# Values of the global attention begun two units at a time behind the first half of the next unit's scores, with five half slots for its probabilities and three packed slots for those of the local attention

## The reference

```python
x = x + _L0_conv_ref(_gn(x), ...)   # global attention
x = x + _L1_conv_ref(_gn(x), ...)   # local attention

# layer 0, per image and head (12 heads of 16 channels, S = 1024 positions)
scores = q @ swapaxes(k) * SCALE + (rel_h + rel_w)      # 1024 x 1024
out = softmax(scores) @ v                               # then w_proj, b_proj

# layer 1: 7 x 7 neighbourhood mask, and 16 registers that every query sees
scores = where(mask_cat, q @ swapaxes(k_cat) * scale, NEG_INF)   # 1024 x 1040
out = softmax(scores) @ v_cat                           # then out_w, out_b
```

## Time and profile before

| | |
|---|---|
| median of 3 runs | 4896.54 us |
| profiled execution | 4902.5 us |
| its span, first to last instruction | 4900.8 us |
| mean granted TensorE clock | 0.951 of full speed |
| TensorE matmuls busy | 4491.2 us, 92% of the span |
| VectorE busy | 3079.3 us, 63% |
| ScalarE busy | 2608.5 us, 53% |
| DMA, mean | 79 GB/s |

### The profile page before, as it was taken

How to read it: one execution, slowest core, us unless ns; L and a number is a source line. 1 busy time by engine, 2 the same in 40 slices (tenths; PEclk the granted TensorE clock), 3 DMA queues, 4 the chain that set the end, 5 groups by cost and what they waited for, 6 DMA issues and landing times.

```text
span 4900.8 us, 97559 instructions
## 1 busy us (share of the span) xinstructions
PE 4491.2 (92%) x32598; PEld 2291.5 (47%) x32598; DVE 3079.3 (63%) x5558; ACT 2608.5 (53%) x3955; POOL 892.5 (18%) x1901
## 2 busy tenths in 40 slices
PE   5879999999999999999999999999999999999998
PEld 3334453544535454453544535455454544535444
DVE  3736667665675656667566675656657566676654
ACT  1533556555564555556555564555646555565564
POOL 3112111222202212121212202212021121102111
PEclk7888999999999999999999999999999999999999
DMA  6334242443414433253433424433144432424401
GB/s 126 83 73 86 49 104 62 99 90 70 89 39 106 87 87 71 53 108 70 99 79 70 88 52 99 94 73 84 44 106 81 99 79 48 101 62 99 87 14 40
DMA packets 235869, 386.05 MB, mean 79 GB/s; under 512 B 58396, under 2 KB 133728, under 8 KB 235360
## 3 DMA queue, kind: packets, MB, share of 16 engines
q1 hardware_dynamic: 189280, 266.13, 23.8%
q10 hardware_dynamic: 21504, 75.51, 7.6%
q0 software_dynamic: 24576, 37.80, 4.8%
HBM read 227.79 MB, written 88.08 MB: 64 GB/s over the span
## 4 chain that ended last, share of the span: by engine, by line
PE 75%; DVE 9%; SPq 5%; issue 5%; DMA 5%; ACT 2%; DVEq 0%; ACTq 0%; POOL 0%
PE P L1135 15%; PE P L1153 14%; PE P L1094 13%; PE P L958 6%; PE P L959 6%; DVE mx L901 5%; PE P L1071 5%; PE P L1185 4%; PE P L1206 4%; PE P L1102 3%; DMA QA<-queries 2%; PE P L1178 1%; SPq L507 1%; DMA biases<-xn 1%; DVE mxc L907 1%
## 5 line engine op out<-in xcount | busy, mean ns | idle before, releaser
L901 DVE TENSOR_REDUCE mx<-P 128x1 f32<-128x512 f32 x3072 | 1923.2, 682 | 471.2 <-PE P L1094 467.9
L771 ACT ACTIVATE probs<-P 128x1024 f32<-128x1024 f32 x1536 | 1507.5, 1022 | 777.7 <-PE P L1153 777.0
L1094 PE MATMUL P<-K,AR 96*128 96x256 f16 x6144 | 1093.1, 282 | 42.9 <-DMA AR<-biases 26.7
L1153 PE MATMUL P<-AR,K 113*128 113x512 f16 x3072 | 924.8, 383 | 14.1 <-DMA AR<-mrow 13.6
L907 DVE TENSOR_REDUCE mxc<-P 128x1 f32<-128x336 f32 (+1 forms) x1536 | 648.2, 474 | 307.6 <-PE P L1103 304.0
L787 ACT ACTIVATE probs<-P 128x320 f32<-128x320 f32 (+3 forms) x1632 | 618.1, 436 | 405.2 <-PE P L1206 340.0
L1135 PE MATMUL P<-probs,V 128*17 128x512 f32 x6144 | 817.2, 604 | 9.9 <-ACT probs L771 9.9
L1094 PEld LDWEIGHTS P<-K,AR 96*128 96x128 f16 x6144 | 541.7, 99 | 566.9 <-DVE mx L901 198.3
L1153 PEld LDWEIGHTS P<-AR,K 113*128 113x128 f16 x3072 | 216.9, 98 | 676.6 <-ACT probs L771 517.8
L1206 PE MATMUL P<-A,K 113*128 113x320 f16 (+2 forms) x1536 | 447.1, 306 | 12.9 <-ACT probs L787 12.1
L1102 PE MATMUL P<-K,A 112*128 112x320 f16 (+1 forms) x1536 | 400.4, 295 | 53.4 <-DVE mx L901 35.8
(11 more groups left out here) (122 smaller groups left out, 3705.4 us busy)
## 6 DMA issues: line engine op xcount, KB each, us to landing
AR<-biases SPq DMA_DIRECT2D x384, 256.0 KB, 7.7
AR<-queries ACTq DMA_DIRECT2D x96, 512.0 KB, 5.8
biases<-xn SPq DMA_DIRECT2D x192, 256.0 KB, 2.9
AR<-queries ACTq DMA_DIRECT2D x96, 256.0 KB, 8.5
K<-oraw POOLq DMA_DIRECT2D x384, 64.0 KB, 4.8
xin<-in_x_dram SPq DMA_DIRECT2D x16, 768.0 KB, 10.5
queries<-oraw SPq DMA_DIRECT2D x384, 32.0 KB, 4.8
QA<-queries SPq DMA_DIRECT2D x192, 64.0 KB, 5.1
```

Source lines behind the costliest of these rows:

```text
L771: nc.scalar.activation(probs[:, u % RING, j:j + 2, :], P[:, b:b + 2, :], ACT.Exp).then_inc(p_done[0], 1)
L901: V_.reduce_max(mx[:, n // 2, n % 2:n % 2 + 1], bank, AX.X).then_inc(used, 1)
L1094: last = mm(bank[:, QD * (v % 2):QD * (v % 2) + QD], AR[0:ROWS_MAX[0], part % SLOTS, v, c, j, 128 * q:128 * q + 128], K0[0:ROWS_MAX[0], h, ...
L1153: last = mm(P[:, j, :], K0[0:ROWS, h, 128 * kt:128 * kt + 128], AR[0:ROWS, p % SLOTS, kt // 2, :, j, :], start=True, stop=True)
```

## The change

1. In the global attention, the values are no longer issued one unit at a time behind a unit's second step. `values_due(step)` says what is due behind a step: behind every fourth step from 4 to 88 (the first step of a unit) the two units before it; behind steps 91, 93 and 95 one unit each; and the last one behind the loop.
2. `probs` is used as half units. `slot_of(step)` gives each step one of five slots up to step 84, four in `probs` and the fifth in `xres`, and one of the four in `probs` from step 85 on. `left_by(step)` is the step whose slot this one takes; ScalarE waits until the values of that step's unit have been used.
3. Since `xres` is lent out, the input image is loaded into it at step 90 in place of step 32, when 43 units have been used (at step 88), and ScalarE waits ahead of the first exponential until the image before has left `xres`.
4. In the local attention `probs` is packed into three slots of the units' true width (PACKED), and the values are issued by `values_due_local(g, u, j)`, behind the first head of a unit: of unit 0 behind unit 2's first head, of units 1 and 2 behind unit 3's, 3 and 4 behind unit 5's, 5 and 6 behind unit 7's, 7 and 8 behind the next group's unit 0.

```diff
-RING = 2
+PACKED = 1280, 1408, 1408
+FIFTHS = 85
+RELOAD = 90
...
+def values_due(step):
+
+    if step % 4 == 0 and 4 <= step < FIFTHS + 4:
+        return [step // 2 - 2, step // 2 - 1]
+    if step % 2 and step > FIFTHS + 4:
+        return [step // 2 - 1]
+    return []
+
+
+def slot_of(step):
+
+    return step % 5 if step < FIFTHS else (step - FIFTHS) % 4
+
+
+def left_by(step):
+
+    return step - 5 if step < FIFTHS + 4 else step - 4
+
+
+def values_due_local(g, u, j):
+
+    if j:
+        return []
+    if u == 0:
+        return [(g - 1, 7), (g - 1, 8)] if g else []
+    return {2: [(g, 0)], 3: [(g, 1), (g, 2)], 5: [(g, 3), (g, 4)], 7: [(g, 5), (g, 6)]}.get(u, [])
...
-                    if kind == "main" and L == 0 and step == STEPS[0] // G:
...
+                    if kind == "main" and L == 0 and step == RELOAD:
+                        sp.wait_ge(pv_done[0], im * UNITS[0] + FIFTHS // 2 + 1)
                         sp.dma_start(xres[:], x_t[im]).then_inc(xres_in, 16)
...
                 if kind == "main" and L == 0:
+                    if not is_image(im, 0):
+                        spilled = im * 16
+                        act.wait_ge(mid_out, spilled)
                     for step in range(STEPS[0]):
                         u, j = step // 2, 2 * (step % 2)
-                        if j == 0 and u >= RING:
-                            act.wait_ge(pv_done[0], im * UNITS[0] + u - RING + 1)
+                        if left_by(step) >= 0:
+                            act.wait_ge(pv_done[0], im * UNITS[0] + left_by(step) // 2 + 1)
                         act.wait_ge(st_done[0], im * STEPS[0] + step + 1)
                         b = 2 * (step % 2)
-                        nc.scalar.activation(probs[:, u % RING, j:j + 2, :], P[:, b:b + 2, :],
+                        nc.scalar.activation(half_unit(step), P[:, b:b + 2, :],
                                              ACT.Exp).then_inc(p_done[0], 1)
...
                         last.then_inc(st_done[0], 1)
                         run_jobs(after[step], 0)
-                    if u:
-                        use(u - 1)
+                        for due in values_due(step):
+                            use(due)
                 use(UNITS[0] - 1)
...
                         run_jobs(after[step], 1)
+                        for dg, du in values_due_local(g, u, j):
+                            use(dg * (TT + 1) + du)
                         step += 1
                     ends.append(step)
-                    if full:
-                        use(full - 1)
+                use(UNITS[1] - 2)
                 use(UNITS[1] - 1)
                 jobs_read(after)
```

More of the change, by code:

```diff
@@ L241, in attention_kernel @@
         vreg = sb("vreg", [128, G, 128])
-        probs = sb("probs", [128, RING, GH, 512])
+        probs = sb("probs", [128, 2, GH, 512])
         onorm = probs[:, 0, 0:3, :].rearrange("p a n -> p (a n)").rearrange("p (t c) -> p t c", t=TT)
@@ L245, in attention_kernel @@
         xres = sb("xres", [128, TT, C])
+        fifth = xres[:].rearrange("p t c -> p (t c)")[:, 0:2 * 512].rearrange("p (j n) -> p j n", j=2)
+        packed = probs[:].rearrange("p a j n -> p (a j n)")
         xn = sb("xn", [128, 2, S])
@@ L288, in attention_kernel, with half_unit, local_unit @@
         P = ctx.enter_context(nc.psum_tensor("P", [128, 8, 512], F32))
+        def half_unit(step):
+            slot = slot_of(step)
+            return fifth if slot == 4 else probs[:, slot // 2, 2 * (slot % 2):2 * (slot % 2) + 2, :]
+        def local_unit(full):
+            heads, at = (GH, sum(PACKED[0:full % 3]))
+            u = full % (TT + 1)
+            if u == 0:
+                heads, width = 2, 512
+            else:
+                width = W * (query_rows(u - 1)[1] - query_rows(u - 1)[0])
+            assert heads * width <= PACKED[full % 3]
+            return packed[:, at:at + heads * width].rearrange("p (j n) -> p j n", j=heads)
         def banks(a, n, rows=128):
@@ L546, in stage @@
                 for step, entries in enumerate(after):
-                    if kind == "main" and L == 0 and step == STEPS[0] // G:
-                        if is_image(im, 0):
-                            sp.wait_ge(rows_in, ROWS_IN)
-                            sp.wait_ge(out_in, 16)
-                        else:
-                            moved, stored = im * 4, im * 16
-                            sp.wait_ge(xT_done[1], moved)
-                            sp.wait_ge(nb_done[1], im)
-                            sp.wait_ge(mid_out, stored)
+                    if kind == "main" and L == 0 and step == RELOAD:
+                        sp.wait_ge(pv_done[0], im * UNITS[0] + FIFTHS // 2 + 1)
                         sp.dma_start(xres[:], x_t[im]).then_inc(xres_in, 16)
@@ L781, in stage @@
                             full = g * (TT + 1) + u
-                            if full >= RING:
-                                act.wait_ge(pv_done[1], im * UNITS[1] + full - RING + 1)
+                            if full >= len(PACKED):
+                                act.wait_ge(pv_done[1], im * UNITS[1] + full - len(PACKED) + 1)
                             for j in range(GH if u else 2):
@@ L786, in stage @@
                                 n = W * (query_rows(u - 1)[1] - query_rows(u - 1)[0]) if u else 512
-                                nc.scalar.activation(probs[:, full % RING, j, 0:n], P[:, step % SCORES[1], 0:n],
+                                nc.scalar.activation(local_unit(full)[:, j, :], P[:, step % SCORES[1], 0:n],
                                                      ACT.Exp).then_inc(p_done[1], 1)
@@ L1135, in use @@
                         last = mm(P[32 * j:32 * j + D + 1, 6, :], V[0][:, kt, GH * (p // 2) + j, :],
-                                  probs[:, u % RING, j, :], start=(kt == 0), stop=(kt == TT - 1))
+                                  half_unit(2 * u + j // 2)[:, j % 2, :], start=(kt == 0), stop=(kt == TT - 1))
                     last.then_inc(pv_done[0], 1)
@@ L1170, in use @@
                     pe.wait_ge(p_done[1], im * STEPS[1] + ends[full])
-                    slot = full % RING
+                    unit = local_unit(full)
                     if full == 0:
@@ L1177, in use @@
                         for half in range(2):
-                            last = mm(P[:, 6 + half, :], vreg[:, g, :], probs[:, slot, half, :],
+                            last = mm(P[:, 6 + half, :], vreg[:, g, :], unit[:, half, :],
                                       start=True, stop=False, skip_group_check=True)
@@ L1185, in use @@
                                 last = mm(P[32 * j:32 * j + D + 1, 6 + half, a - 512 * half:b - 512 * half],
-                                          V[1][:, u - 1, GH * g + j, :], probs[:, slot, j, a - lo:b - lo],
+                                          V[1][:, u - 1, GH * g + j, :], unit[:, j, a - lo:b - lo],
                                           start=False, stop=(u == HALF_UNITS[half] - 1), skip_group_check=True)
```

## The result

| | before | after |
|---|---|---|
| median | 4895.58 us (4 runs, 4892.41 to 4898.04) | 5116.85 us (4 runs, 5109.57 to 5127.25) |
| profiled execution | 4902.5 us | 5109.57 us |
| its span | 4900.8 us | 5107.0 us |
| mean granted TensorE clock | 0.951 | 0.941 |

The change makes the kernel slower: ratio 1.0454, 95% interval 1.0434 to 1.0473, or 221 us between the medians. The forecast was 5062 us (4925 to 5125) and slower. The two profiled executions lie 207 us apart; the other 14 are in the medians. One profiled execution of the experiments, that of the changed kernel with cheaper reductions, fell in a slow state (5522.9 us at a granted clock of 0.741), so no row of it is read.

What follows compares the result with a forecast made beforehand. TensorE (92% busy) and VectorE wait for each other; a pair's absence outlasts VectorE's 1.41 us of stored work. Terms 2.5 + 3.2 + 0.6 + 0.4 + 3.6 = 10.3 us per image, 165 us for 16: 5062 us, range 4925 to 5125.

Steps and rivals of the forecast that it cites:

- Part 1: Switch between value and score matmuls: each pair saves 0.21 us of TensorE, 34 round trips or 7.1 us per image.
- Part 2: Global attention, six pairs in steps with two layer 0 jobs: VectorE idles 1.31 us per pair, +0.41 each, +2.5 per image.
- Part 3: Pairs behind steps 44, 60, 76, directly behind a transpose: VectorE idles 2.97 us, +1.07 each, +3.2 us per image.
- Part 4: Pairs behind steps 80, 84, 88, two layer 1 jobs: saved switch lost waiting for exponentials, +0.2 each, +0.6 us per image.
- The sign that was named: In steps with layer 1 jobs, four steps should take 5.4 us.
- Part 5: Ten pairs behind steps 4 to 40 of the global attention: +0.4 us per image, bounds -2.1 and +4.1.
- Part 6: Local attention: eight pairs +2.4, pair behind the middle transpose +1.2, together +3.6 us per image; bounds -2.5 and +8.3.
- Image 0 and the last local attentions: Image 0 should lose a little more, the last two local attentions a little less; taken to cancel.
- The switches decide: Rival: TensorE is 92% busy, so saved switches make the whole kernel 114 us faster, 4783 us; 8%.
- The mixed steps absorb it: Rival: Part 2 to Part 4 as worked out, Part 5 and Part 6 at lower bounds, 4924 us; 13%.
- The clock: Rival: longer TensorE idle time lowers the granted clock, 2 us more lost behind five transposes per image, 5222 us; 6%.
- The prediction's own test: Prediction wrong if the granted clock falls in the earlier trace's steps with two layer 0 jobs, where it was 1.00.

## Why the prediction was right, and where its sizes were off

The direction and the mechanism are shown. The loss is in the order alone (the run with new buffers and old order: ratio 0.9998), it shrinks to 50 us when VectorE's reductions are cheap, and the opposite order is faster. By the parts, per image, from the distances of scores four steps apart (means of 12 loop turns):

| part | forecast | measured |
|---|---|---|
| 2, six pairs in steps with two layer 0 jobs | +2.5 | +1.7 |
| 3, three pairs behind a transpose | +3.2 | +3.4 |
| 4, steps with two layer 1 jobs, with the shift of the first values | +0.6 | +0.6 |
| 5, ten early pairs | +0.4 | +1.8 |
| 6, local attention | +3.6 | +5.3 |
| sum | 10.3 | 12.8 |

*Part 1, the switch.* A pair takes 1.84 or 1.85 us wherever the clock is full, so the seam between its units costs nothing, and one round trip less per pair stands as worked out from the earlier trace rows. It reached the time nowhere that a run could tell: even with half of the reductions' columns the change lost 50 us.

*Part 2.* VectorE's gap was forecast at 1.31 us and the period at 6.25; the rows show 1.30 and 6.17, and the means of the six distances 5.85 to 6.77 (before 5.84 to 6.43). The gap behind every pair stands as forecast; the +0.41 per pair was 0.28 on average. Behind step 52 nothing is lost (5.84 before, 5.85 after); why wasn't studied.

*Part 3.* 2.97 us forecast and 2.97 read. The transposes' pairs lose 1.56, 1.04 and 0.76 us, in place of 1.07 each.

*Part 4.* The steps from 80, 84 and 88 lose 0.59, 0.10 and 1.02 us; the four first steps gain 1.08 by the later start of the values. The sum agrees, the parts don't, so the agreement is luck. The sign that was named, 5.4 us for four such steps, was met by none of the three: 5.77, 5.28 and 6.20.

*Part 5 is the first mis-sized term.* It was put at +0.4 with bounds of -2.1 and +4.1. The measured 1.8 is mostly the four steps from 12 (8.73 before and 10.24 after), so mostly the clock. Their pair runs at 1.2 GHz and takes 3.50 us from start to scores in the turn shown (2.34 to 3.55 in the others), up to 1.7 more than at the full clock:

```profile
1998.36 2.05 PE L1115 MATMUL P<-QA,Z 128*128 128x64 f16 x16
...
2002.05 1.04 PE L1179 MATMUL P<-probs,V 128*17 128x512 f32 x2
...
2005.55 0.60 PE L1197 MATMUL P<-AR,K 113*128 113x512 f16 x2
```

Ahead of it stand position terms of 64 columns each (L1115), and by the records the clock fell at 1998.61, while they ran. This loss is the clock and not VectorE: where the clock stayed full, these four steps took 8.31 us before (six images) and 7.96 with pairs (two images of the run with global pairs alone), so the pair would have gained 0.35. Before, a unit's values behind step 11 lost up to 0.85 at the low clock (1.84 in place of 0.99) in ten of 16 images; the pair loses up to twice that, and in all 16. The sum had no term for the clock; it stood among the rivals alone.

*Part 6 is the second.* The pairs of 320 columns cost VectorE 0.50 us and not 0.38, and the one behind the transpose runs at the low clock in half of the turns: the four steps from 60 lost 1.9 us in place of 1.2. With TensorE kept at work ahead of it, they take 4.10 us in every turn, in place of 4.10 to 5.59, and 4.10 is 1.26 more than before (2.84), so that the 1.2 was right where the clock is full.

*Image 0 and the last local attentions.* These were let cancel. Image 0's global attention lost 14.9 us, 7.5 more than the others; the last two local ones lost nothing.

The account from the forecast of 165 to the measured 221: global parts +12, image 0 +8, local +17, the rest of the program +4; that is the 206 us between the profiled spans. The remaining 15 are that after's profiled run was its fastest and before's was 7 us over its median. The measured 5116.85 lies 8 us below the end of the stated range. That it lies inside is in part luck: the range was built without the clock, which had a share in what was missed.

*The rivals.* "The switches decide" falls with all runs. "The mixed steps absorb it" falls with parts 5 and 6, which lost 1.8 and 5.3 us and gained nothing. The clock was given as a rival by which the time would be 5222; its size was wrong, but its mechanism acts beside the main one: 125 us more at 1.2 GHz, of which TensorE's filled waits gave 69 back, and 31 us of time. The prediction's own test, a granted clock that falls in the steps of the earlier trace rows, was the wrong place: it is 1.00 there after the change too, and the falls lie behind transposes and position terms. The Trainium skill, "TensorE: Matmul & The Clock Gate", section A second HAM failure mode, says that short idle times of TensorE between groups of matmuls can make the clock swing. The trace agrees behind some waits of 1.5 to 2.1 us, but not behind the same 1.47 us in seven of 14 turns or the 1.56 us at 2085.48, and not in the steps of the earlier trace rows with 0.19.

How much of the 221 us is the clock as a whole isn't settled, but it can be bounded by estimates. From below: filling the waits for transposes gave 31 us. From above: some 125 us more at 1.2 GHz would have taken at least half as long at 2.4 GHz, so the extra low clock costs at most some 63 us. By that the rest, 158 us or more, is not the clock, and the run with cheap reductions ties it to VectorE. A version without the falls behind position terms wasn't tried.

## What to carry to other kernels

When two engines hand work to each other through few buffers, count what the other one has stored at the moment when this one turns away, and keep each absence shorter than that. Here three banks held 1.41 us, one absence was 1.85, and joining two absences into one saved 0.21 us of switching and lost more than that nearly everywhere; moving the short absences to where the store is full made the kernel 3.0% faster with the same instructions. The engine that is 92% busy is not the only bound if it and a neighbour wait for each other in turn: here saving the busy engine's time made the kernel slower, and halving the reductions of the engine that was 63% busy made it 3.4% faster. Make the neighbour's work cheaper in one run and see how far both move.

## What the hardware showed that was not expected

- A switch between value matmuls and score matmuls costs 0.21 us per round trip (worked out from the earlier trace rows), and a seam between two groups of values costs nothing: pairs take 1.85 us, which is 2 x 0.87 and 0.11, with nothing between.
- A wait of about 1.5 us can double the time of the matmuls behind it, but needn't: a local pair took 2.26 us in place of 1.21 behind a wait of 1.47 us, in seven of 14 turns with that same wait, and a global one 2.64 in place of 1.85 behind a wait of 2.13 us. Useless matmuls in the waits for transposes made the kernel 31 us faster.
- The clock also falls with TensorE at work: it fell during position terms of 64 columns each, and the pair of values behind them took up to 3.55 us in place of 1.85.
- With values between the jobs the local attentions, in which nothing was changed, took 18 us longer in all. The time at 1.2 GHz rose too, from 484 to 521 us, but mostly elsewhere; TensorE's waits for the transfer into `QA` rose from 45.4 to 67.3 us, mostly in the steps that got longer.
